# A new order of steps in every engine's program of a four-layer attention network, and fewer semaphore waits on TensorE

## What is computed

```python
def L0(tgt, memory, mask):            # 16 heads of 16
    t = layer_norm(tgt, g1, be1)
    tgt = tgt + self_attention(t, mask) @ Wo.T + memory @ Wg.T
    return tgt + relu(layer_norm(tgt) @ W1.T) @ W2.T
def L1(ctx, x):                       # one head of 256, no projections
    f, n = layer_norm(x), layer_norm(ctx)
    h = gelu(attention(f, n, n) @ fc1.T); cross = h @ fc2.T
    return f + gamma2 * (cross + gamma1 * attention(norm(cross), norm(cross), norm(cross)))
def L2(q, ctx):                       # 16 heads of 16, causal
    a = layer_norm(attention(q, ctx, ctx) + q)
    return gelu(a @ W1.T) @ W2.T + a
def L3(x, ctx, prog):                 # 8 heads of 32, then a recurrence over the 128 tokens
    x = x + attention(norm(x), norm(ctx)) @ Wo.T
    u = (norm(x) @ W_in.T) @ Bmat
    s_t = silu(s_{t-1} @ A.T) + u_t   # t = 0..127
    return x + s @ Cmat + mean(prog) @ W_prog.T
```

## Time and profile before

| what | value |
|---|---|
| median of 3 runs | 937.99 us (936.37 to 939.94) |
| profiled execution, its own time | 936.61 us |
| span from its first to its last instruction | 934.5 us |
| TensorE busy | 765.0 us, 82% |
| VectorE busy | 550.1 us, 59% |
| ScalarE busy | 443.9 us, 48% |
| GpSimd busy | 336.5 us, 36% |
| mean granted TensorE clock | 0.907 of full speed |

### The profile page before, as it was taken

How to read it: one execution, slowest core, us unless ns; L and a number is a source line. 1 busy time by engine, 2 the same in 40 slices (tenths; PEclk the granted TensorE clock), 3 DMA queues, 4 the chain that set the end, 5 groups by cost and what they waited for, 6 DMA issues and landing times.

```text
span 934.5 us, 16718 instructions
## 1 busy us (share of the span) xinstructions
PE 765.0 (82%) x5520; PEld 617.2 (66%) x5520; DVE 550.1 (59%) x2244; ACT 443.9 (48%) x1776; POOL 336.5 (36%) x343
## 2 busy tenths in 40 slices
...
DMA packets 14710, 18.75 MB, mean 20 GB/s; under 512 B 3485, under 2 KB 12194, under 8 KB 13986
## 3 DMA queue, kind: packets, MB, share of 16 engines
...
...
## 4 chain that ended last, share of the span: by engine, by line
PE 60%; DVE 18%; ACT 10%; issue 6%; SPq 2%; POOL 2%; DMA 2%; DVEq 0%; POOLq 0%
PE work_bank L536 19%; PE work_bank L545 18%; ACT probs L1063 6%; PE scores_bank L744 5%; PE work_bank L674 4%; DVE probsT L985 3%; PE scores_bank L572 3%; DVE xn L902 3%; ACT probs L1126 3%; PE work_bank L594 2%; DVE stats L921 2%; PE work_bank L528 2%; DVE probs L884 2%; DMA bias<-in_mask 2%; PE work_bank L666 1%
## 5 line engine op out<-in xcount | busy, mean ns | idle before, releaser
L767 POOL TENSOR_TENSOR probs<-probs,rtotal 128x512 f32<-128x512 f32 x160 | 165.6, 1044 | 209.9 <-DVE rtotal L975 208.3
L1063 ACT ACTIVATE probs<-probs,nmx 128x128 f32<-128x128 f32 x512 | 197.9, 390 | 54.8 <-DVE nmx L884 54.5
L545 PE MATMUL work_bank<-L_w,hidden 128*128 128x256 f32 x512 | 114.8, 383 | 1.6 <-issue 1.0
L985 DVE COPY probsT<-work_bank 128x512 f32<-128x512 f32 x160 | 104.7, 681 | 11.5 <-PE work_bank L674 10.6
L767 POOL TENSOR_TENSOR rstd<-veps,half 128x2 f32<-128x2 f32 x64 | 44.8, 699 | 184.7 <-DVE veps L929 183.8
L545 PEld LDWEIGHTS work_bank<-L_w,hidden 128*128 128x128 f32 x512 | 97.2, 192 | 15.2 <-issue 1.6
L674 PE MATMUL work_bank<-ident,probs 128*128 128x128 f32 x640 | 94.1, 287 | 15.9 <-POOL probs L767 9.9
L674 PEld LDWEIGHTS work_bank<-ident,probs 128*128 128x128 f32 x640 | 73.8, 146 | 36.3 <-POOL probs L767 19.3
L1063 ACT ACTIVATION_READ_ACCUMULATOR probs<-probs,nmx 128x1 f32 x512 | 96.6, 189 | 0.0
L528 PE MATMUL work_bank<-ident,xn 128*128 128x128 f32 x256 | 42.6, 287 | 48.0 <-DVE xn L902 45.9
L744 PE MATMUL scores_bank<-probs,a_t 64*64 64x16 f32 x252 | 49.5, 275 | 33.4 <-ACT probs L1126 33.4
...
## 6 DMA issues: line engine op xcount, KB each, us to landing
...
```

The source lines that it names most:

```text
L545: mm = nc.tensor.matmul(d[:, b * D:b * D + D], xT, w, start=(n == 0), stop=(n == len(todo) - 1))
L767: return nc.gpsimd.tensor_tensor(out, a0, a1, op)
L985: nc.vector.tensor_copy(turn_slot(s, i, key), d[:].rearrange("p (j k) -> p j k", j=4))\
L1063: ins = nc.scalar.activation(e_at[slot][:, j, :], src, ACT.Exp, bias=nmx[:, slot, j:j + 1], scale=1.0 if s == "C" else -1.0, accum_out=tot ...
```

## The change

All steps stay, and so do the load order and all arithmetic. The steps stand in another order in all four tables. On TensorE semaphore waits are left out where an earlier wait of the same program already covers them (`ready` remembers the highest value waited for of each semaphore), and where several fills are drained by one engine, only the last of them in that engine's order is waited for (`emptied_last`). Printed, TensorE's program names 1307 semaphores waited for before and 882 now. ScalarE's program held 32 loads of an activation table before and holds 24 now.

```diff
 TENSOR_ORDER = """
-H0.flip.x G0.flip.c H0.k H0.q H0.v A0.score.0 G0.flip.cn G0.v1 H1.flip.x A0.turn.0 A0.score.1 A0.turn.1 H1.k A0.turn.2
+G0.flip.c H0.flip.x G0.flip.cn H0.k H0.v H0.q A0.score.0 G0.v1 A0.score.1 A0.turn.0 A0.turn.1 A0.turn.2 A0.turn.3
...
 SCALAR_ORDER = """
...
-B7.flip.x4 B7.q C6.q B7.exp.0 B7.exp.1 B7.exp.2 B7.exp.3 C6.exp.0 C6.exp.1 C6.exp.2 K7.k C6.exp.3 B7.exp.4 B7.exp.5
...
+EMPTIED = {e: {x: n for n, x in enumerate(program(e)) if x in FILL_AT} for e in "da"}
...
+        def emptied_last(fills):
+
+            out = []
+            for e in "da":
+                mine = [x for x in fills if x in EMPTIED[e]]
+                if mine:
+                    s, i, step = max(mine, key=EMPTIED[e].get)
+                    out.append(done(s, i, *step))
+            return out
...
+            waited = {}
+
+            def ready(of, n):
+
+                if waited.get(of.name, 0) < n:
+                    waited[of.name] = n
+                    pe.wait_ge(of, n)
...
-                    pe.wait_ge(drained[n % W_BANKS], n // W_BANKS)
+                    ready(drained[n % W_BANKS], n // W_BANKS)
...
-                for j in range(4):
-                    pe.wait_ge(*done(s, i, "turn", first + j))
-                pe.wait_ge(*done(KEYS[s], i, "v"))
+                for at in emptied_last([(s, i, ("turn", first + j)) for j in range(4)]):
+                    ready(*at)
+                ready(*done(KEYS[s], i, "v"))
...
-                    for m in range(FC // 2):
-                        pe.wait_ge(*done(s, i, "ffn1", m))
+                    for at in emptied_last([(s, i, ("ffn1", m)) for m in range(FC // 2)]):
+                        ready(*at)
```

More of the change, by code:

```diff
@@ L49 @@
[L49 to L88, removed]
@@ L90 @@
+C6.flip.x7 B7.ffn1.1 C6.drive B7.ffn2 C7.flip.x6 C7.q C7.score C7.turn.0 C7.turn.1 C7.turn.2 C7.turn.3 C7.mix C7.out
+C7.flip.x7 C7.drive
 """
 VECTOR_ORDER = """
-G0.bias G1.bias H0.stat.x H0.norm.x G0.stat.c H0.flip.x G0.norm.c H0.v H1.stat.x A0.max.0 H1.norm.x A0.max.1 A0.rec.0
-A0.max.2 A0.max.3 A0.rec.1 A0.turn.0 A0.rec.2 H1.flip.x A0.max.4 A0.rec.3 A0.turn.1 A0.max.5 A0.turn.2 A0.turn.3
-A0.rec.4 A0.max.6 A0.mix.0 A0.rec.5 A0.max.7 A0.rec.6 A0.turn.4 G2.bias A0.turn.5 A0.rec.7 A0.turn.6 A0.turn.7
@@ L161 @@
[L161 to L164 removed]
+H0.stat.x G0.bias G0.stat.c H0.norm.x G0.norm.c H0.flip.x H0.v A0.max.0 A0.max.1 A0.max.2 A0.max.3 A0.rec.0 A0.rec.1
@@ new lines @@
+A0.max.4 A0.turn.0 A0.rec.2 A0.turn.1 A0.max.5 A0.rec.3 A0.max.6 A0.turn.2 A0.rec.4 A0.max.7 A0.turn.3 A0.rec.5
+A0.turn.4 A0.rec.6 A0.mix.0 A0.rec.7 H1.stat.x A0.turn.5 A0.turn.6 H1.norm.x G1.bias A0.turn.7 G2.bias H1.flip.x J0.v
+A0.mix.1 A0.out A0.stat.x2 H1.v A0.norm.x2 A0.flip.x2 A1.max.0 A1.max.1 A1.max.2 A1.max.3 A0.ffn1.1 A1.rec.0 A0.ffn1.0
+A1.rec.1 A0.ffn1.2 A1.rec.2 A0.ffn1.3 A1.rec.3 A1.turn.0 A1.turn.2 A1.turn.1 A1.max.4 A1.turn.3 A1.max.5 A1.max.6
+A1.rec.4 A1.max.7 G3.bias A1.rec.5 A1.rec.6 A0.ffn2 A1.rec.7 A1.turn.4 M0.stat.x3 A1.turn.5 A1.turn.6 M0.norm.x3
@@ new lines @@
+A1.mix.0 A1.turn.7 M0.flip.x3 H2.stat.x A1.mix.1 M0.max.a G1.stat.c M0.rec.a H2.norm.x G1.norm.c H2.flip.x A1.out
+M0.turn.a A1.stat.x2 A1.norm.x2 H2.v A1.flip.x2 A1.ffn1.1 M0.stat.cr A1.ffn1.0 M0.norm.cr A1.ffn1.2 A2.max.0
+M0.flip.cr A2.max.1 A2.max.2 A2.max.3 A2.rec.0 A1.ffn1.3 M0.max.s A2.rec.1 A2.max.4 A2.turn.0 A2.max.5 M0.rec.s
+A2.max.6 A2.rec.2 A2.rec.3 A2.rec.4 A1.ffn2 M1.stat.x3 A2.rec.5 M0.turn.s A2.turn.2 A2.rec.6 A2.turn.3 M0.self
+A2.turn.1 A2.max.7 M1.norm.x3 G4.bias A2.turn.4 A2.turn.5 H3.stat.x M1.flip.x3 A2.rec.7 H3.norm.x A2.mix.0 B0.max.0
```

327 lines of the change are left out of this document (179 added, 148 removed).

## The result

| what | before | after |
|---|---|---|
| median of 6 runs | 938.11 us | 903.68 us (898.54 to 905.01) |
| profiled execution, its own time | 936.61 us | 904.56 us |
| span | 934.5 us | 902.4 us |
| TensorE busy | 765.0 us, 82% | 762.0 us, 84% |
| mean granted TensorE clock | 0.907 | 0.905 |

What follows compares the result with a forecast made beforehand. TensorE was taken as the bound in the middle, with other waits and chains at start and end. Terms -14.3 - 3 - 4 - 4 - 10.5 - 0.5 = -36.3 gave 900.3 us profiled, about 902 median; range 885 to 924.

Steps and rivals of the forecast that it cites:

- The mask at the start: First pair: its statistics no longer queue behind pair 1's mask on VectorE; first norm at 21.0 instead of 35.32: -14.3 us.
- I count it as nothing: New head, `G0.flip.cn` ahead of `H0.k`: costs 0.6 us more, saves `G0.flip.c` and a later stall; counted as 0.
- Filling: `A1.score.0` to `B0.score.0`: less of layer 1's chain is waited for directly; -3 us, bounds -8 and +3.
- Middle: Four periods from `B1.score.0` to `B5.score.0`: less time lost per pair in the new order; -4 us, bounds -9 and +10.
- The two new stalls: Middle pairs: TensorE waits 2.2 us before `M.score.a` for turn 4's bank, 2.0 before `B.flip.o` through the mask, pairs 3 to 5.
- Pairs 5 and 6: Layer 2, `B5.score.0` to `B7.score.0`: A7 is half a pair ahead; walk some 150 us, discounted to -4, bounds -8 and +2.
- B7 and C6: `B7.score.0` to `B7.ffn2`: `B7.score.1` follows early and exps run without a break; -10.5 us, bounds -14 and -3.
- Fewer waits: TensorE's left-out waits: at most 0.06 us for three or four waits in dense stretches; -0.5 us in the sum.
- Only the start: Rival: only the start's 14.3 us come back, middle and end settle on other waits of the same size; 923.7 us, chance 0.14.
- Every wait: Rival: each of 425 waits left out on TensorE returns 0.06 us, -26 on top; 876 us, chance 0.04.
- The clock takes the end back: Rival: TensorE stays near 1.2 GHz from `B7.score.0` to `B7.ffn2`, -10.5 becomes about -2; 910 us, chance 0.08.
- VectorE in every pair: Rival: VectorE's new order holds TensorE, 5.2 us more per pair if stalls add up; 951 us at 7, chance 0.04.

Runs made afterwards that it cites:

- that edit alone: The kernel before with only the second pair's mask bias moved on VectorE behind A0's first four maxima: 924.48 us, ratio 0.9855.
- the ten profiles with the new orders: Profiles of the changed kernel and its variants; from `B5.score.0` to `B7.score.0` they lie between 148.4 and 151.6 us.
- only the tail new: The kernel before up to B7's scores, then the change's order on all four engines from there on: 930.32 us, ratio 0.9919.
- the second set: Side-by-side repetition: the changed kernel once more, 906.48 us, and the changed kernel with all of TensorE's waits as before, 909.70 us.

## Why the prediction was right, and where not

- **The mask at the start** (-14.3): the flip 14.2 earlier, and 14.35 with that edit alone. That GpSimd is late next was right too. The step "I count it as nothing", for the steps up to `A1.score.0` (forecast at about 65, measured 68.8), failed: 2.9 us are lost there, 2.1 of them as longer busy time at a lower clock (0.63 from 36 to 52 us). The move alone loses 1.8 there.
- **Filling** (-3, measured +3.9, and +1.6 on to `B1.score.0`): the term was mis-sized and has the wrong sign; 3.9 lies inside none of its bounds (-8 and +3). The walk gave 9.8 us lost, measured are 16.7. Of the 6.9 missed, 2.4 are pair 4's mask, which the walk did not count (shown by moving it), and 1.7 are `A1.out` at half clock (so in three of the ten profiles with the new orders, at full clock in seven). The other 2.8 are small waits without one cause. The discount for waits that a walk doesn't see was in the right direction and much too small. The size of the miss is that of this pair of profiles: the old order took 73.4 to 76.7 us here in four profiles, the changed kernel 77.3 in two. So nothing was gained, and the loss is anything from 0.6 to 3.9 us.
- **Middle** (-4, measured -4.9): the number is right by luck. With all waits kept the four periods take 355.7 and 356.3 us, so the new order by itself gives about 1 us of the 4.9 and the fewer waits the rest. The sum also counts 2.0 us for the first period as if it had no mask, which it has; by its own figures (79.1 + 8.8 + 1) nothing is gained there, and measured are 3.3. The two new stalls, though, stand where they were put and have their sizes (2.2 forecast, 2.15; 2.0 forecast, 2.2, 2.1 and 3.2), and the second is gone after the last mask. Not foreseen: the longest of them costs 1.1 us more in the step behind it, at half clock.
- **Pairs 5 and 6** (-4, measured -8.9): the walk said some 150 us, measured are 148.4, and 148.4 to 151.6 in the ten profiles. So the term is -6 to -9, and the discount was the error. No run tells its parts.
- **B7 and C6** (-10.5, measured -12.4; -9.5 with only the tail new): the mechanism right, `B7.mix.1` 3 us later than walked, and less lost to the clock than the 4 us that I kept.
- **Fewer waits** (-0.5, bounds 0 and -3): mis-sized. The dense stretches cost nothing, as the argument said, and the mixes in dry places do, as it said too; but in the new order it is 3.2 and 5.3 us and not 0.5, beyond the term's bound. In the old order there is no gain (+1.6).
- **The rivals.** Only the start: 924 is indeed what the start alone gives, so the other 21 us refute it. Every wait: refuted at 26 us, though some waits are paid. The clock takes the end back: not so, the stage takes 40.0 to 42.0 us in all ten profiles. VectorE in every pair: its stall is there in each of five pairs, but it is 2.15 us and not 5.2 or 7, and the periods as a whole are shorter than before, save the third.

Of the signs named ahead, `A1.score.0` at 65 us failed, and two of the four periods (85.5 and 90.7) lie outside 87 to 89, though inside the 85 to 91 that would have refuted it; the others came true.

That the median came out within 2 us is partly luck. Up to `B1.score.0` the kernel lost 11.5 us more than the terms said, and from there on it gained 7.9 more. Like for like, the profiled execution was forecast at 900.3 and took 904.6. The median was put 1.4 us above it and fell 0.9 below; in the second set it was 906.5.
